# Gathers in fours behind their landing, the next unit's x1 in mid-slot, the first unit's C tiles by halves

## What is computed

```python
e = jnp.stack([tbl_0[ids[:, 0]], ..., tbl_23[ids[:, 23]]], axis=1)      # 1024 x 24 x 16
# each layer, with Xk = e at first and W of shape (24 * H_prev, 64):
Xk = jnp.einsum('bfd,bhd,fho->bod', X0, Xk, Wr)                          # 64 maps of 16
outs.append(Xk.sum(axis=2))
...
h = jnp.concatenate([z, dense_ctx], axis=1)                              # 192 + 16
h = jnp.maximum(h @ W_top1 + b_top1, 0.0)
h = jnp.maximum(h @ W_top2 + b_top2, 0.0)
y = h @ W_top3
```

## Time and profile before

| | |
|---|---|
| time, median of 3 runs | 481.65 us (480.46 to 482.58) |
| profiled execution, its own time | 481.3 us |
| its span, first to last instruction | 479.5 us |
| TensorE busy | 399.4 us, 83% |
| VectorE, GpSimd, ScalarE busy | 289.4, 192.7, 116.1 us |
| mean granted TensorE clock | 0.939 |

### The profile page before, as it was taken

One profiled execution on the slowest core, in us unless ns is written; L12 is line 12 of the kernel. 1 busy time (PEld: TensorE's weight loads), 2 busy tenths in 40 slices (PEclk: granted clock), 3 DMA queues, 4 the chain that ended last, 5 costly groups with the idle time before them and its releaser, 6 DMA issues.

```text
span 479.5 us, 5682 instructions
## 1 busy us (share of the span) xinstructions
PE 399.4 (83%) x2246; PEld 159.9 (33%) x2246; DVE 289.4 (60%) x275; ACT 116.1 (24%) x261; POOL 192.7 (40%) x196
## 2 busy tenths in 40 slices
PE   0061221699899999999999999999999999999977
PEld 0050000333333333443434234433342344334355
DVE  1011000199697897777777778686869786866500
ACT  1000000003143132423231323232323331423332
POOL 5777777066474665545453645363000000000000
PEclk9995555699999999999999999999999999999989
DMA  3168970096777959574956496459545873000000
GB/s 89 18 143 185 231 165 7 2 221 164 168 137 180 218 94 248 131 169 74 229 113 173 79 222 167 122 92 213 156 119 94 204 191 85 11 1 0 1 1 2
DMA packets 57357, 58.93 MB, mean 123 GB/s; under 512 B 38673, under 2 KB 44305, under 8 KB 57330
## 3 DMA queue, kind: packets, MB, share of 16 engines
q1 hardware_dynamic: 51186, 56.97, 49.8%
q0 software_dynamic: 6144, 1.59, 4.1%
HBM read 56.43 MB, written 2.10 MB: 122 GB/s over the span
## 4 chain that ended last, share of the span: by engine, by line
PE 80%; issue 15%; another core or an unknown queue 3%; ACT 1%; DMA 0%; SPq 0%
PE ps_x L301 46%; PE ps_b L301 14%; PE ps_tower L301 9%; PE ps_turn L301 5%; PE ps_tower L307 3%; PE ps_turn L346 2%; PE ps_turn L354 1%; ACT G L507 0%; DMA id_sb<-ident 0%; ACT x_rows L487 0%; ACT x_sb L477 0%; ACT x_sb L482 0%; ACT h L533 0%; ACT h L540 0%
## 5 line engine op out<-in xcount | busy, mean ns | idle before, releaser
L278 DVE TENSOR_TENSOR Z<-A,ps_b 128x1024 f32<-128x1024 f32 x192 | 223.1, 1217 | 73.5 <-PE ps_b L301 49.0
L157 POOL DMA_INDIRECT x_rows<-tbl,ids_sb x192 | 192.5, 1003 | 139.3 <-DVE Z L278 72.5
L301 PE MATMUL ps_x<-Z,w_sb 128*64 128x512 f32 x768 | 188.8, 602 | 0.0
L271 DVE TENSOR_TENSOR Z<-A,C 128x1024 f32<-128x1024 f32 x48 | 56.6, 1221 | 42.8 <-issue 28.7
L301 PE MATMUL ps_b<-x_sb,pick_sb 64*128 64x512 f32 x256 | 72.0, 640 | 0.0
L301 PEld LDWEIGHTS ps_x<-Z,w_sb 128*64 128x64 f32 x768 | 46.2, 136 | 75.0 <-issue 59.2
L307 PE MATMUL ps_tower<-id_sb 128*128 128x128 f32 x86 | 16.5, 332 | 58.7 <-issue 58.7
L301 PE MATMUL ps_x<-Z,w0s_sb 128*64 128x512 f32 x192 | 50.6, 618 | 12.3 <-issue 12.3
L494 ACT ACTIVATE x_diag<-ps_turn,mask_sb 128x192 f32<-128x192 f32 x128 | 50.8, 608 | 39.5 <-PE ps_turn L354 36.8
L477 ACT COPY x_sb<-ps_x 128x512 f32<-128x512 f32 x16 | 9.4, 586 | 143.0 <-PE ps_x L301 136.7
L283 DVE TENSOR_REDUCE z_q<-x_sb 128x32 f32<-128x512 f32 x16 | 10.9, 679 | 45.3 <-ACT x_sb L477 45.3
(11 more groups left out here) (32 smaller groups left out, 95.6 us busy)
## 6 DMA issues: line engine op xcount, KB each, us to landing
A<-x_scratch SPq DMA_DIRECT2D x48, 512.0 KB
C<-x_scratch SPq DMA_DIRECT2D x48, 512.0 KB
x_rows<-tbl,ids_sb POOLq DMA_INDIRECT x192
x_quarters<-x_scratch SPq DMA_DIRECT2D x16, 128.0 KB
x_scratch<-x_rows SPq DMA_DIRECT2D x7, 192.0 KB
w_sb<-w SPq DMA_DIRECT2D x2, 384.0 KB
x_scratch<-x_rows SPq DMA_DIRECT2D x11, 64.0 KB
wt_sb<-wt SPq DMA_DIRECT2D x1, 512.0 KB
```

Source lines behind the costliest of these rows:

```text
L157: pool.indirect_dma_start(out=x0_rows[t % 2][:, f * D:(f + 1) * D], out_offset=None, in_=tables[f], in_offset=bass.IndirectOffsetOnAxis(ap ...
L271: nc.vector.tensor_tensor(Z[s % ZR][:, :], A[u % AS][i][:, :], C[i][:, :], ALU.mult).then_inc(z_ready, 1)
L278: nc.vector.tensor_tensor(Z[s % ZR][:, :], A[u % AS][i][:, :], ps_b[j % 2][:, :], ALU.mult)\
L301: return nc.tensor.matmul(out, lhsT, rhs, start=start, stop=stop)
```

## The change

- **Gathers.** `BURST = 4`. GpSimd waits until the last part of tile 0 has landed before tile 1's first gather. From tile 1 on, each fourth gather waits until all earlier gathers on its tile's semaphore have landed. Tile 1 waits for no products, and gather f of tile t from 2 on for 15(2t - 4) + 30f/24 products, one slot later than before.
- **x1 in mid-slot.** VectorE, TensorE and ScalarE handle x1 of unit u + 1 after product 5 of unit u instead of ahead of product 0. `turn_x2` follows product 0, and VectorE's `sum_x1` follows product 9 instead of 5. In the count of products x1 of the next unit now stands between products 5 and 6.
- **Unit 0's C by halves.** A C tile's 128 partitions hold 8 features of part i and 8 of the next. Each half is a transfer of its own and goes out when its part is stored: behind part i, the lower half of C i, the upper half of C i - 1, and A i.
- **Warm-up and tower weights.** `WARM` goes from (40, 8, 8, 30) to (40, 16, 16, 4). The tower's weights are loaded behind unit 3's tiles, not behind unit 1's.

```diff
-WARM = (40, 8, 8, 30)
+WARM = (40, 16, 16, 4)
+BURST = 4
...
-    return i + 1 if u == 0 else NI + PER_SLOT * (u - 1) + i + 1
+    return i + 1 if u == 0 else NI + PER_SLOT * (u - 1) + NP2 // 2 + i + 1
...
-    return NI + PER_SLOT * u + (NI if u + 1 < UNITS else 0) + n + 1
+    return NI + PER_SLOT * u + (NI if u + 1 < UNITS and n >= NP2 // 2 else 0) + n + 1
...
+            pool.wait_ge(gathered_part[NI - 1], 16 * FR)
             for t in range(1, TILES):
                 if t >= 2:
                     wait_stored(pool, t - 2)
                 for f in range(F):
 
-                    after(pool, z_ready, PER_SLOT * (2 * t - 5) + 2 * PER_SLOT * f // F)
+                    if t >= 2:
+                        after(pool, z_ready, PER_SLOT * (2 * t - 4) + 2 * PER_SLOT * f // F)
+                    if f % BURST == 0:
+                        after(pool, gathered[t % 2], 16 * (F * ((t - 1) // 2) + f))
                     gather(t, f, gathered[t % 2])
...
+            def load_c_half(u, i, g):
+
+                src = rows_of(u, FR * (i + g), FR).rearrange("t f c -> (t f) c").unsqueeze(1)
+                half = C[i][HR * FR // 2 * g:HR * FR // 2 * (g + 1), :]
+                sp.dma_start(half, src.to_broadcast([FR, FR, COLS])).then_inc(C_in[i], 16)
...
-                if i == 1:
-                    sp.wait_ge(part_stored[0], STORES)
-                    load_a(0, 0)
-                    sp.wait_ge(part_stored[1], 16)
-                    load_c(0, 0)
-                    load_a(0, 1)
-            sp.wait_ge(part_stored[2], 16)
-            load_c(0, 1)
-            load_a(0, 2)
-            load_c(0, 2)
+                sp.wait_ge(part_stored[i], STORES if i == 0 else 16)
+                load_c_half(0, i, 0)
+                load_c_half(0, (i - 1) % NI, 1)
+                load_a(0, i)
...
             for u in range(UNITS):
-                if u + 1 < UNITS:
-                    for i in range(NI):
-                        cross1(u + 1, i)
                 for n in range(NP2):
                     cross2(u, n)
                     if n == 5 and u + 1 < UNITS:
+                        for i in range(NI):
+                            cross1(u + 1, i)
+                    if n == 9 and u + 1 < UNITS:
                         sum_x1(u + 1)
```

More of the change, by code:

```diff
@@ L439, in slot @@
                         make_b(u, 3)
+                        if u + 1 < UNITS:
+                            for i in range(NI):
+                                cross1(u + 1, i)
                     if n == 6:
```

22 lines of the change are left out of this document (10 added, 12 removed).

## The result

The changed kernel takes **515.29 us** (514.02 to 516.19, 4 runs), the kernel before 482.12 (480.46 to 482.74, 4 runs): **1.069 times as long**, 95% interval 1.065 to 1.073. The forecast was 464 us, 3.7% faster, with a range of 442 to 486; the time lies outside it and has the other sign. The profiled execution has a span of 511.9 us and a mean granted clock of 0.937, as against 479.5 and 0.939 before.

What follows compares the result with a forecast made beforehand. Bound by the crawl until 95.97 us, then TensorE's work to 479.5. With the crawl gone, gathers bind by a hair: tile 7's landing 366.4 + 22.6 + 73.6 + 1.8 = 464.4, forecast 464 us, range 442 to 486.

Steps and rivals of the forecast that it cites:

- The crawl: TensorE's single instructions 2.8 us apart at half clock, before 95.97 us; forecast to go; rival that it stays 10%.
- something that gathers fill in 33.6 us and that drains afterwards: Crawl's supposed cause: draining keeps up with gathers in up to about 87% of the time; fours make 83%.
- The gain it set out from, 44 us: Start: without the crawl the first slot begins at about 52 us, where it was 95.97.
- The landing under load: GpSimd's wait at each fourth gather: 5.5 us to land while tiles travel, 1.3 otherwise.
- Fewer gathers in time: Tile 1's gathers: bursts of 10.2 or 6.0 us, landed by 79.9, x1 of unit 2 done on TensorE at 102.5.
- an estimate that it didn't follow: Gathers' landings at 2.0 us unloaded: some 12 us more over seven tiles, 476 us.
- The slow rival: Tile periods: gathers become the bound, slower than before above 49.7 us a tile; 52 gives 498 us; 15%.
- C by halves: Unit 0's loads: product 1 stays at 42.68, product 2 starts at 44.9; one of two 2.25 us shares saved.
- Tile 1: Its gathers begin at 35.7 us, end landed at 79.9, and are stored and loaded again by 85.1.
- The prediction's 18 us: TensorE standing at unit 1's mid-slot for x1 of unit 2, wanted at 84.5 us, done at 102.5.
- x1 in mid-slot and tower weights: Between 0 and 0.3 us a slot, taken as 0; the weights' 6 us transfer only lengthens the time of late landings.
- What would show it: Signs: no clock fives from 50 us, stores 47 to 49 us apart; growing A and C waits mean the slow rival.

Runs made afterwards that it cites:

- a_old_gathers: Changed kernel with the kernel before's gathers, no wait for a landing: 476.1 us, kernel before 481.9.
- d_before: The kernel before, unchanged, run again in another group for its trace: 483.9 us, kernel before there 480.7.
- b_first_pause: Kernel before plus one wait of GpSimd, for the landing of tile 0's gathers: 452.7 us, kernel before there 451.6.
- e_three_pauses: Changed kernel with tile 1's landing waits only after its 8th, 16th and 24th gather, later tiles held by products: 455.4 us, 1.007 of before (451.3).
- e_whole_c: Changed kernel, tile 1's gathers in three eights, later tiles held by products, unit 0's C tiles loaded whole as before: 451.9 us, kernel before 451.3.
- b_two_pauses: Kernel before with new gathers: landing waits only after tile 0 and tile 1's 12th and 24th gather, later products gate: 461.0 us, before 451.6.
- e_rests: Kernel before, GpSimd filling an unused tile with zeros after each 8 gathers of tiles 1 and 2, no landing wait: 453.8 us, before 451.3.
- c_two_pauses: Changed kernel with landing waits only after tile 0 and tile 1's 12th and 24th gather: 453.8 us, kernel before 451.6.
- c_fours_lag: Changed kernel, each four gathers waiting for the landing of the four before the last four: 450.9 us, kernel before 451.6.
- f_whole_c: Changed kernel, tile 1 in three eights, unit 0's C whole, on a chip with the crawl: 463.1 us, 0.966 of before (479.4).

## Why the prediction was wrong

**The crawl goes: right, for a wrong reason, and so by luck.** The clock row has no run of fives, 16 transposes take 3.4 us and the first slot begins at 58.67 instead of 95.97. But the account of it (something that gathers fill in 33.6 us and that drains afterwards) is refuted three times: the onset moves from the 27th gather to the 43rd in a_old_gathers; with an empty queue TensorE crawls on (d_before); and with 97 gathers in a row, on another chip, b_first_pause shows none. The prediction had itself named the second of these against it, "from 72 on ... gathers can't have been queued for long", and gave it 10%. What it couldn't see from one trace is that two of the four chips tried don't show the crawl at all. The gain it set out from, 44 us, can only be had on the others, and there the whole crawl is worth some 26 to 30 us.

**The landing under load: the step that failed.** It stands in "Fewer gathers in time": "A burst costs 3.75 + 0.95 + 5.5 = 10.2 us then and 6.0 otherwise". Measured are 13.4 and 7.1. Of the difference for a loaded four, 1.2 us is the landing (6.7 for 5.5), 0.5 are gathers that take 1.6 to 2.0 us, and 1.5 is a term that was not in the sum at all, the time from the landing to the next gather's start; for an unloaded one that is 1.10. (The 1.3 us of the unloaded landing had it in, but for SyncE, which goes on 0.35 us after the landing at 13.88.) Part of it cancelled, since the forecast's fours ("bursts then land at 15, 26, 34.5 to 36") had three slow ones a tile and the trace two: three of 10.2 and three of 6.0 are 48.6, two of 13.4, three of 7.1 and one of 5.0 are 53.1. The forecast had 49 + 5 x 47.5 = 286.5 us for the six periods from tile 1 to tile 7, the stores have 323.6: 37 of the 51 us that were missed. 11 more are tile 1's, stored at 91.14 for 79.9.

The Trainium skill (DMA: Bandwidth & Descriptors, Anatomy of one DMA) had 2.0 us of fixed cost, and the prediction used it for an estimate that it didn't follow. Unloaded, the runs have 1.10 + 1.10 = 2.20 us from a gather built to the next gather's start, the wake-up included, nearer to it than the row's 1.3; loaded it is 8.2, and no fixed figure holds.

**The margin.** The slow rival was worked out with its break-even, 49.7 us a tile against a forecast of 47.2, and given 15%. A margin of 2.5 us in a sum of six landings, each of which I had from one row, was worth more than that: 0.4 us more on each was enough. The rival's own price (52 us a tile, 498) was short too, by 1.9 us a tile.

**C by halves: wrong sign.** "Product 1 stays there" (42.68) and "product 2 starts at 44.9" became 50.32 and 52.42. The changed order sends part 1's loads at 28.80, ahead of the landing of tile 0's last gathers, which then land 3.7 us later (38.33 for 34.59; 4.6 in e_three_pauses against e_whole_c), and part 2 is stored at 39.49 instead of 35.75. From that store to product 1 it is 10.8 us, not 6.9: the copies, halves first, move 103 GB/s from 41.6 to 46, where the old order moved 187 from 38 to 42.7. The first slot began at 58.67 for the 52 of the forecast. Undone alone it gives 3.5 us back (e_three_pauses, e_whole_c; one execution of the latter). The term was costed by bytes; what it moved ahead of the gathers was left out.

**Tile 1: the shape right, the sizes late.** It started at 39.73 for 35.7 (the halves), was stored at 91.14 for 79.9, and x1 of unit 2 had its first product at 107.92. TensorE stood 19.6 us and had x1 of unit 2 contracted at 115.0. The prediction's 18 us ran from the time at which x1 would have been contracted without a wait (84.5) to the time at which it was (102.5); measured, these are 92.4 (89.7 and 2.7) and 115.0, so 22.6 us: the demand came 8 us later than worked out, the supply 12.5.

**x1 in mid-slot and tower weights: right within their bounds.** From the first make_b of unit 5 to that of unit 15 TensorE does the same 1,364 matmuls in either order, and no tile is late. With x1 at the slot's start they take 237.67 us (before, b_first_pause, b_two_pauses, e_rests), in mid-slot 238.12 (e_whole_c, c_two_pauses, c_fours_lag): 0.05 us a slot, at the lower end of "between 0 and 0.3", where the prediction had put it. It pays at one place, unit 2, where b_two_pauses waits 7.4 us longer than c_two_pauses. In all, the rest of the change is worth 5 to 7 us by three pairs of mostly single executions (476.1 for 481.9; 453.8 for 461.0; and 515.3 for 519.9, whose kernels before, in two groups, agree within 0.3 us).

**What would show it** pointed the right way: the wait for A came back in every second slot, as the prediction had written for the slow rival (23.65, 12.85, 6.22, 7.43 us ahead of the first products of units 2, 4, 6, 8, and 10.28, 7.53, 9.20 of units 10, 12, 14). It didn't grow, as the sign asked; it stayed, and the stores' distance, 53.9 us for "47 to 49", told more plainly.

## What to carry over

A wait for one's own DMA ahead of each issue costs the whole round, building, landing under the load of that moment, and waking up, and it is to be priced at the busiest moment of its cycle, not the quiet one: here 8.2 us for 2.2. Leaving one group in flight (c_fours_lag) still holds the gathers back and takes 100.8 us of waiting for landings down to 19.7.

A stall that one trace shows may belong to the chip that it was taken on. Before a change is built on it, the unchanged kernel should be run on several; here it was 451 us on two and 479 to 484 on the other two, a difference of 6%, where 3.7% had been forecast for the change. And a stall's length isn't its price: the crawl held the first slot back by 43 us and cost some 26 to 30, since the next waits stood right behind it.

To compare two orders of the same work, measure between marks that enclose the same instructions in both. Between the first products of x1 of units 5 and 15 the two orders differ by 2.6 us (233.1 and 235.7), but these marks stand half a slot apart in the two kernels and enclose unequal work; between marks with equal work they differ by 0.45.

No version beat the kernel before everywhere. f_whole_c is 3.4% faster where the crawl shows, and its twin e_whole_c no different where it doesn't (451.9 for 451.3).
